# Head attention: ScalarE takes over the copy of the values, and its copies of q move to the end of its loop

## What is computed

```
x = x + attn(layernorm(x))          # B, S, D = 8, 64, 512; H = 16 heads; hd = 32
  qkv = x @ Wqkv.T + bqkv
  qkv = qkv.reshape(B, H, S, 3 * hd)        # no transpose: 16 x 64 rows out of 64 x 16 pieces
  q, k, v = jnp.split(qkv, 3, axis=-1)
  scores = jnp.einsum('bhsd,bhtd->bhst', q, k) * (1.0 / math.sqrt(hd))
  attn = jax.nn.softmax(scores, axis=-1)
  vals = jnp.einsum('bhst,bhtd->bhsd', attn, v).reshape(B, S, D)
  return vals @ Wo.T + bo
```

## Time and profile before

| | us |
|---|---|
| Median of 3 runs (931.84 to 937.68) | 935.09 |
| The profiled execution: its own time | 930.46 |
| The profiled execution: span of its records | 928.7 |
| `head_attention` in it, from its first to its last instruction | about 725.3 to 800.4 |
| Busy in the span: PE / DVE / ACT / POOL | 773.4 / 599.4 / 364.7 / 162.1 |

### The profile page before, as it was taken

The page is one execution under the profiler, slowest core; times in us unless marked ns, Lnnn a source line. Parts: engine busy times, 40 slices in busy tenths (PEclk is TensorE's granted clock), DMA queues, the critical chain, the costliest instruction groups (busy, mean ns, idle before and its releaser), DMA issues. The chain is left out here.

```text
span 928.7 us, 37863 instructions
## 1 busy us (share of the span) xinstructions
PE 773.4 (83%) x17278; PEld 645.3 (69%) x17278; DVE 599.4 (65%) x1146; ACT 364.7 (39%) x726; POOL 162.1 (17%) x431
## 2 busy tenths in 40 slices
PE   3598679998989998989997989978589787659995
PEld 1445669998978997978997978878545665324442
DVE  2777447784775785876775875645565787893225
ACT  3577414432444433534333531111247664452221
POOL 3020210402130411220411220201001103240003
PEclk9899789999999999989999999989879798879998
DMA  9947990227093336092346091510394711454424
GB/s 340 357 103 140 233 203 4 55 55 201 5 162 145 55 61 196 15 192 103 54 65 192 12 178 52 110 32 13 127 354 117 233 25 24 155 168 96 126 80 147
DMA packets 179419, 115.75 MB, mean 125 GB/s; under 512 B 145788, under 2 KB 158132, under 8 KB 176060
## 3 DMA queue, kind: packets, MB, share of 16 engines
q1 hardware_dynamic: 168272, 100.85, 43.0%
q10 hardware_dynamic: 8988, 6.69, 2.4%
q0 software_dynamic: 2000, 5.80, 2.1%
HBM read 61.94 MB, written 12.85 MB: 81 GB/s over the span
## 5 line engine op out<-in xcount | busy, mean ns | idle before, releaser
L1021 PE MATMUL banks<-qa,ctxT 128*128 128x64 f16 x3744 | 121.5, 195 | 22.0 <-issue 12.8
L1021 PEld LDWEIGHTS banks<-qa,ctxT 128*128 128x128 f16 x3744 | 117.6, 100 | 24.4 <-issue 14.2
L972 PEld LDWEIGHTS banks<-wall,whhT 128*128 128x128 f16 x3456 | 111.7, 100 | 15.9 <-issue 8.8
L972 PE MATMUL banks<-wall,whhT 128*128 128x64 f16 x3456 | 114.0, 195 | 9.0 <-issue 7.5
L972 PE MATMUL banks<-qa,wall 128*128 128x64 f16 x3456 | 104.9, 193 | 3.1 <-DVE qa L783 2.8
L972 PEld LDWEIGHTS banks<-qa,wall 128*128 128x128 f16 x3456 | 102.5, 98 | 3.4 <-DVE qa L783 3.0
L1040 PE MATMUL banks<-qa,wall 128*128 128x64 f16 (+1 forms) x1872 | 92.5, 198 | 8.4 <-issue 6.7
L1040 PEld LDWEIGHTS banks<-qa,wall 128*128 128x128 f16 (+1 forms) x1872 | 91.6, 102 | 9.4 <-issue 9.4
L1040 PE MATMUL banks<-wall 128*128 128x64 f16 (+1 forms) x936 | 91.3, 198 | 2.1 <-issue 2.1
L1040 PEld LDWEIGHTS banks<-wall 128*128 128x128 f16 (+1 forms) x936 | 86.6, 102 | 1.9 <-issue 1.9
L88 POOL TENSOR_TENSOR wall<-wall 128x64 f32<-128x64 f32 x24 | 12.3, 512 | 363.7 <-DVE wall L83 363.7
(11 more groups left out here) (280 smaller groups left out, 1495.6 us busy)
## 6 DMA issues: line engine op xcount, KB each, us to landing
wall<-in_ctx_dram SPq DMA_DIRECT2D x17, 1024.0 KB, 10.3
wall<-in_L_ffn_routed_w_dram SPq DMA_DIRECT2D x23, 512.0 KB, 8.2
unit<-in_ctx_dram SPq DMA_DIRECT2D x6, 1024.0 KB, 7.6
xg_scratch<-room SPq DMA_DIRECT2D x1, 3840.0 KB, 20.3
y_scratch<-room ACTq DMA_DIRECT2D x15, 256.0 KB, 2.1
ctxT<-in_L_xattn_gru_wih_dram SPq DMA_DIRECT2D x3, 1024.0 KB, 17.5
ctxT<-in_L_xattn_gru_whh_dram SPq DMA_DIRECT2D x1, 3072.0 KB, 25.9
ctxT<-in_L_attn_Wqkv_dram SPq DMA_DIRECT2D x12, 256.0 KB, 8.0
```

The lines of the kernel that those rows point to most:

```text
L972: mm = pe.matmul(dst[o], a, b, start=start, stop=True, skip_group_check=True)
L1021: mm = pe.matmul(score[n][:, t * K:(t + 1) * K], a, q, start=(k == 0), stop=(k == 3 * DC - 1), skip_group_check=True)
```

## The change

Three edits, all in `head_attention`:

1. `values_out`, the two copies of a group's values out of PSUM, is no longer in DVE's list but in ACT's, as two ACT copies of the same shapes. In iteration k ACT does it for group k - 1, behind the exponentials of group k + 1; for group 7 it stands behind the loop.
2. `q_block(k + 2)` goes from the head of ACT's iteration to behind `values_out(k - 1)`, ahead of `v_block(k + 2)`.
3. DVE's list is otherwise as it was.

```diff
@@ ACT
+            def values_out(k):
+                for j in range(2):
+                    act.wait_ge(valued, 2 * k + j + 1)
+                    t0 = 64 * k + 32 * j
+                    dst = vals[:, :, t0:t0 + 32].rearrange("e c (m r) -> e m c r", r=4)
+                    act.copy(dst, value[0:HD, j, :].rearrange("e (m c r) -> e m c r", c=HC, r=4)).then_inc(vals_out, 1)
...
             for k in range(B):
-                if k + 2 < B:
-                    q_block(act, h, qT, k + 2)
                 v_in(k)
                 probs_turned(k)
                 if k + 1 < B:
                     exponentials(k + 1)
+                if k >= 1:
+                    values_out(k - 1)
                 if k + 2 < B:
+                    q_block(act, h, qT, k + 2)
                     v_block(k + 2)
                 if k >= 3 and k % 2 == 1:
                     vals_high((k - 3) // 2)
                 if 2 <= k < B - 1:
                     wall_high(act, e_all, IN_PROJECT + k - 2, IN_PROJECT + k - 1)
+            values_out(B - 1)
             act.wait_ge(vals_out, 4 * RT)
@@ DVE
-            def values_out(k):
-                for j in range(2):
-                    dve.wait_ge(valued, 2 * k + j + 1)
-                    t0 = 64 * k + 32 * j
-                    dst = vals[:, :, t0:t0 + 32].rearrange("e c (m r) -> e m c r", r=4)
-                    dve.tensor_copy(dst, value[0:HD, j, :].rearrange("e (m c r) -> e m c r", c=HC, r=4)).then_inc(vals_out, 1)
...
                 if k >= 5 and k % 2 == 1:
                     add_y((k - 5) // 2)
-                if k >= 1:
-                    values_out(k - 1)
                 if k >= 3 and k % 2 == 1:
                     vals_low((k - 3) // 2)
                 if k >= 3:
                     wall_low(dve, e_all, IN_PROJECT + k - 3, IN_PROJECT + k - 2)
-            values_out(B - 1)
             add_y(RT - 2)
```

## The result

The changed kernel takes 952.31 us (median of 4 runs, 951.70 to 955.58); the kernel before, measured beside it, 936.38 (931.84 to 942.46). The ratio, taken over the runs of both kernels, is 1.0232, 95% interval 1.0203 to 1.0261: slower by 2.3%, 21.7 us on the median of 935.09 shown at first. It isn't the quotient of the two medians, which is 1.017 (15.9 us), and how it weighs the single runs isn't known here. The four executions of the kernel before scatter by 10.6 us here; its 39 executions beside the experiments have medians of 929.3 to 933.0, and against those 952.31 is 1.021 to 1.025. So the loss is clear, and its size is known to some us only. Predicted were 955.5 us, 20.4 us more than before, in a range from 944 to 964.

The account below looks back on a forecast made before the run. In the head attention DVE slightly paced some groups, a chain through ACT's order or PE's list others. Waits 11.9 plus clock 8.5 made 20.4 us: 950.9 on the profiled execution, 955.5 after its 4.6 offset; range 944 to 964.

Parts of the forecast that it names:

- PE waits for q: Before the scores, PE stands still 3.49 us in each of groups 1 to 5, 2.4 in group 0.
- The steps at the higher clock: Times between successive groups' starts of turning probabilities, the last to add_y's end; clock high from 736: +11.9 us in sum.
- step 0: From group 0's turn of probabilities to group 1's: +1.3 us with the clock rising at 736.0, otherwise a further +1.9.
- Step 7: From group 7's turn of probabilities to add_y of tile 2: +1.10 us, vals_high waiting behind two copies of values.
- The clock's term: PE's granted clock falling after the new gaps in the loop: 1.9 us plus four falls at 1.65, 8.5 us.
- steps 3 and 5: From turning probabilities of groups 3 and 5 to the next group's: vals_high behind values and q, +2.16 us each.
- The clock that stays high: Rival: PE's clock in the loop stays up after the new gaps; 947.0 us, chance 0.17.
- The clock that stays low: Rival: PE's clock stays low through the whole loop; +45 us in all, 980, chance 0.06.
- The relief of DVE: Rival: DVE's list bounds all eight groups, so its copies come off; -10.5 us, 924.6, chance 0.03.
- A q that isn't late: Rival: q isn't late where it counts, only vals_high moves back; +2.5 us, 937.6, chance 0.07.
- Behind the loop: After the head attention's loop, up to the barrier, nothing is lost or won.
- gaps of 0.4 cost nothing: PE's 0.4 us waits in the loop leave the clock up: it stayed at 1.00 from 736 to 756.

Follow-up runs that it names:

- e2: Against the kernel before: q_block moved behind ACT's exponentials, values still copied by DVE; ratio to before 1.0191.
- e7: The change plus 10 (group 0) or 31 (groups 1 to 5) unread fp16 products on PE ahead of its wait for q; ratio to before 1.0113.
- e4: The change plus 8 (group 0) or 22 (groups 1 to 5) unread unit-matrix turns on PE ahead of its wait for q; ratio to before 1.0146.
- e1: Against the change: q_block back at the head of ACT's iteration, values still copied by ACT; ratio to before 1.0069.
- e5: Against the kernel before: in DVE's list, vals_low of tiles 0 and 1 moved behind the norms of groups 4 and 6; ratio to before 0.9915.
- e6: Against the kernel before: values copied by ACT, q_block still at the head, vals_low moved behind the next norm in DVE's list; ratio to before 0.9960.
- e8: Against e5: DVE's copies of values put ahead of add_y; ratio to the kernel before 0.9941.
- e3: Against the change: q_block put ahead of the copies of values in ACT's list; ratio to the kernel before 1.0201.
- e9: Against the change: vals_low moved behind the next norm in DVE's list; ratio to the kernel before 1.0246.

## Why the prediction was right

*PE waits for q.* Shown. The median of 952.31 us lies 3.2 below the forecast, and the mechanism is the one forecast. 3.49 us were predicted for groups 1 to 5 and 2.4 for group 0; the trace has 3.40 to 3.52 and 2.40. e2 has the wait without the moved copies, and most of the loss with it.

*The cost of an ACT copy of the values.* Taken as 0.586 by the nearest row; it is 0.573 in the median of the 16:

```profile
L1528 ACT COPY wall<-banks x16: 568/573/574, 743.6 to 806.4; 32x512 f32<-32x512 f32 x16
```

*The steps at the higher clock.* The prediction beside e7, where the clock was kept up, and the change itself:

| step | before | predicted, clock high | e7 | the change |
|---|---|---|---|---|
| 0 | 7.96 | 9.3 | 7.91 | 10.54 |
| 1 | 5.29 | 8.13 | 8.18 | 10.59 |
| 2 | 5.16 | 8.13 | 8.17 | 10.41 |
| 3 | 7.78 | 9.94 | 9.80 | 10.27 |
| 4 | 8.88 | 10.83 | 12.29 | 12.96 |
| 5 | 7.78 | 9.94 | 9.80 | 10.55 |
| 6 | 8.75 | 6.19 | 6.09 | 6.09 |
| 7 | 8.04 | 9.14 | 10.83 | 9.16 |

Steps 1, 2, 3, 5 and 6 are right to 0.14 us. In steps 4 and 7 of e7 the clock fell; in step 0 it came back 3.3 us after the mark, so the step took 7.91 and not 9.3. That goes with a filler: in e4 it was 3.9 us, without a filler 6.5 to 7.5 where q is copied in advance (before, e1, e5, e6, e8) and 10.0 to 10.3 where it is late (the change, e2, e3, e9).

Step 7 can be read in the change itself: 9.16, as summed, but the path isn't quite the one summed. The prediction gave the 1.10 to `vals_high`, and had the wait for the copied values hidden. In group 7, which has no q, nothing hides it: PE waits 1.42 us for ACT's first copy, and the projection starts right behind PE's own products, with `vals_low` done at 806.19, 0.14 us earlier. Both paths had grown by the same two copies, so the number came out.

```profile
804.85 0.62 ACT L1532 CAST ctxT<-unit 128x512 f16<-128x512 f32 x1
805.50 0.69 DVE L1594 TENSOR_TENSOR ctxT<-unit,ctxT 128x512 f16<-128x512 f32 x1 [2.87 <-ACT ctxT L1532]
806.33 2.76 PE L1674 MATMUL banks<-room,ctxT 128*128 128x512 f16 x12
```

*The clock's term.* 8.5 us were predicted: 1.9 in step 0, and four falls of 1.65. The change minus the prediction at the higher clock is 1.3, 2.5, 2.3, 0.3, 2.1 and 0.6 for steps 0 to 5: 9.1. The sum is nearly right, the parts are not. All five gaps of groups 1 to 5 brought a fall, not four (in group 0 the clock was low already, and came back later), and a fall costs 2.1 to 2.5 us where all of PE's work is on the chain (steps 1, 2, 4). The cheaper price from the kernel before, 3.3 us at half clock, was the wrong row to take: here each stretch at 0.50 lasts 6 to 7 us with 4.5 to 5.6 us of PE work in it, half of which is the loss.

```profile
744.30:750.60 6.30, 4.88 (x46) 0.50 0.04 9
754.30:761.00 6.70, 4.69 (x46) 0.50 0.20 42
764.40:771.40 7.00, 4.80 (x46) 0.51 0.00 0
```

What made up for it is steps 3 and 5: there PE's slower round, 10.3 and 10.6, lies beside DVE's chain of 9.9 (9.80 in e7), so a fall costs only 0.3 and 0.6. The prediction had priced the falls as if all of them were on the chain, and by e9 they no longer are. The two errors nearly cancel; that the clock's term is off by only 0.6 us is luck.

The Trainium skill, TensorE: Matmul & The Clock Gate, "HAM oscillation — how this bites in real kernels", has the clock throttled again in every turn of such a loop. The trace agrees: in groups 1 to 5 there are five gaps and five falls. The count by that rule was right; the 10.2 us that the prediction worked out from it are 1.1 above the 9.1 in the table, its own 8.5 are 0.6 below, and both used the wrong price and left out the overlap in steps 3 and 5.

*The rivals.* The clock that stays high: 947.0; e7 shows what that would have been, 1.0113 or about 946. The clock that stays low: it came back in each step. The relief of DVE: DVE gave up 10.6 us of work and its waits grew; e6 has ACT's copies within a time below that of before, but only after a chain was cut that the change left in place. A q that isn't late: out, by the waits.

*Behind the loop.* From the end of `add_y` of tile 2 to the first instruction of `experts` it was 12.6 us before and is 12.6 after, as predicted.

## What to carry to other kernels

An engine with low busy time has room, but its instructions still stand in a row: before moving work onto it or within it, count from the moment its input arrives to the moment when the most urgent output of the row leaves, and look who waits for that one. The copy of q made in advance cost PE no wait here; the same copy behind the critical ones was on the chain, and cost more (1.9%, e2) than the work that was moved (0.7%, e1). And where a chain through another engine makes PE idle in each turn of a loop, add the clock: by the ratios of e7 and the change it about doubled the price of the waits (1.2% on top of 1.1%), by the loops of their profiles it was 7.5 of 20.9 us.

## What was not expected of the hardware

- Idle stretches of 2.3 to 2.45 us in each group (e2, e3) brought the clock down about as much as those of 3.4 to 3.5 us: steps of 9.9 and 10.0 us with a clock of 0.65 to 0.67, for 10.6 and 10.4 with 0.68 and 0.67.
- Shorter waits were not safe either, and the same wait didn't always do the same. PE's wait of 1.42 us for the copied values in group 7 stands before a fall in e2, e4 and e7, and before none in the change, e1, e3, e6 and e9. In e8 the clock fell from 749.6 to 753.0 though PE had waited at most 0.39 us at a time since the clock rose at 736; the kernel before, with the same list in that stretch and the same 12.1 to 12.2 us busy from 736 to 749.5, kept 1.00. So "gaps of 0.4 cost nothing" in the prediction holds for the kernel before and not for all.
- PE kept busy by turns of a unit matrix (e4: 8.61 of 9.74 and 8.13 of 9.26 us busy in steps 1 and 2) did not hold the clock at 1.00 in the profiled execution; two of its other three executions had the mean clock and the time of e7. The fp16 products (e7: 8.04 of 8.18 and 8.03 of 8.17) held it there in steps 1 and 2. Whether the kind of work or the 1.13 us of idle that e4 left before the scores made the difference was not tried.
- Outside the loop executions differ by more than the smaller effects: the head attention began at 718.9 to 727.2 us in the profiles, and `experts` took 127.1 to 131.7. Marks within the loop of one profile agreed with the sums to 0.14 us where the clock was high; the medians of kernels whose loops differ by 3 us (e5, e6, e8) did not follow the loops.
